# Gate products in two GpSimd steps, the next unit's normalisation at the iteration's end

## The reference, cut to what matters

```python
# block 0, per batch: m = silu(cond) @ w_ada + b_ada, split in nine shifts, scales and gates
h = ln(x) * (1 + sc_msa) + sh_msa
h = windowed_self_attention(h)                  # 16 heads of 16, windows of 128, rolled by 64
x = x + h * g_msa
h = ln(x) * (1 + sc_mca) + sh_mca
h = topk_cross_attention(h, context)            # 77 context rows, softmax over the 16 largest scores of each head
x = x + h * g_mca
h = ln(x) * (1 + sc_mlp) + sh_mlp
a, b = split(h @ w_m1 + b_m1)                   # 1024 each
x = x + (silu(a) * b @ w_m2 + b_m2) * g_mlp
# block 1: layer norm, attention to 77 prototypes, three experts (silu), router, gate
nx = layer_norm(x); ev = softmax(nx Wq (P Wk)^T) P Wv
routed = sum_e p_e * (silu([nx, ev, anchor] @ e_w1) @ e_w2 + e_b2)
x = x + sigmoid(silu([nx, ev, anchor] @ gate_w1) @ gate_w2) * (routed @ out_w + out_b)
```

## Time and profile before

| what | value |
|---|---|
| timed runs | 1451.67, 1452.09, 1446.48 us (median 1451.67) |
| profiled execution | 1447.34 us, span 1445.5 us |
| busy: TensorE / its weight loads | 97% / 81% |
| busy: VectorE / ScalarE / GpSimd | 73% / 56% / 30% |
| chain that ended last | TensorE 59%, VectorE 31%, issue 5%, ScalarE 2%, GpSimd 1% |
| mean granted TensorE clock | 0.992 |
| spacing of the full iterations | 81.3 to 89.9 us |

### The profile page before, as it was taken

How to read it: one execution, slowest core, us unless ns; L and a number is a source line. 1 busy time by engine, 2 the same in 40 slices (tenths; PEclk the granted TensorE clock), 3 DMA queues, 4 the chain that set the end, 5 groups by cost and what they waited for, 6 DMA issues and landing times.

```text
span 1445.5 us, 29891 instructions
## 1 busy us (share of the span) xinstructions
PE 1402.6 (97%) x9585; PEld 1174.8 (81%) x9585; DVE 1061.5 (73%) x4754; ACT 815.8 (56%) x2523; POOL 439.9 (30%) x600
## 2 busy tenths in 40 slices
PE   7999999999999999999999999999999999999997
PEld 5878788888888788888888788888888878887886
DVE  3576869687786868879696787959688786968632
ACT  3473474747566375755647366564757547474433
POOL 1414132333224233332335132233334313232302
PEclk9999999999999999999999999999999999999999
DMA  7610000000010000010010000000010000000000
GB/s 244 207 64 2 1 8 19 9 27 9 20 32 16 1 2 25 1 34 9 19 33 1 16 1 16 11 23 13 8 34 19 16 2 7 3 1 9 1 2 14
DMA packets 32760, 35.29 MB, mean 24 GB/s; under 512 B 8744, under 2 KB 27868, under 8 KB 32349
## 3 DMA queue, kind: packets, MB, share of 16 engines
q1 hardware_dynamic: 32605, 33.38, 7.6%
HBM read 28.83 MB, written 4.22 MB: 23 GB/s over the span
## 4 chain that ended last, share of the span: by engine, by line
PE 59%; DVE 31%; issue 5%; ACT 2%; POOL 1%; SPq 0%; DMA 0%; DVEq 0%; POOLq 0%; ACTq 0%
PE bank L1033 10%; DVE knocked L2264 10%; PE bank L964 9%; PE bank L1009 7%; PE bank L824 6%; PE bank L1016 4%; DVE M L2257 4%; DVE M L2252 4%; PE bank L873 4%; PE bank L973 3%; PE bank L863 2%; PE bank L810 2%; DVE scores L2272 2%; PE bank L885 2%; DVE gT L2279 2%
## 5 line engine op out<-in xcount | busy, mean ns | idle before, releaser
L964 PE MATMUL bank<-hB,Wm 128*128 128x256 f32 x1024 | 244.0, 384 | 2.2 <-ACT hB L1404 2.2
L964 PEld LDWEIGHTS bank<-hB,Wm 128*128 128x128 f32 x1024 | 191.8, 191 | 33.8 <-issue 7.0
L1009 PE MATMUL bank<-nxT,W1nx 128*128 128x256 f32 x896 | 212.5, 383 | 0.0
L1443 ACT ACTIVATE prob<-bank,rmax 128x128 f32<-128x128 f32 x512 | 179.9, 435 | 28.1 <-DVE rmax L2191 28.1
L1801 POOL TENSOR_TENSOR scores<-scores,M 128x308 f32<-128x308 f32 x128 | 94.8, 741 | 318.4 <-DVE knocked L2264 317.1
L1033 PE MATMUL bank<-W2p,gT 128*128 128x256 f32 x768 | 183.2, 381 | 3.0 <-DVE acc L2343 1.9
L1009 PEld LDWEIGHTS bank<-nxT,W1nx 128*128 128x128 f32 x896 | 166.5, 191 | 23.2 <-issue 2.8
L1033 PEld LDWEIGHTS bank<-W2p,gT 128*128 128x128 f32 x768 | 141.2, 190 | 23.8 <-issue 2.8
L1493 ACT ACTIVATE tbs<-bank,b1half 128x256 f32<-128x256 f32 x128 | 60.6, 473 | 145.0 <-PE bank L964 103.9
L1443 ACT ACTIVATION_READ_ACCUMULATOR prob<-bank,rmax 128x1 f32 x512 | 140.7, 276 | 0.0
L1509 ACT ACTIVATE tbs<-bank,betaH 128x256 f32<-128x256 f32 x224 | 95.1, 486 | 80.1 <-PE bank L1016 79.1
(11 more groups left out here) (240 smaller groups left out, 2800.7 us busy)
## 6 DMA issues: line engine op xcount, KB each, us to landing
Wm_g<-in_L_xcond_w_m_dram SPq DMA_DIRECT2D x4, 1024.0 KB, 5.5
W1ev<-in_L_xcond_e_w_dram SPq DMA_DIRECT2D x6, 512.0 KB, 7.6
x<-in_x_dram SPq DMA_DIRECT2D x16, 128.0 KB, 2.5
x<-in_x_dram SPq DMA_DIRECT2D x32, 64.0 KB, 2.4
Wm<-in_L_xcond_w_m_dram SPq DMA_DIRECT2D x1, 2048.0 KB, 9.2
out_dram<-acc SPq DMA_DIRECT2D x16, 128.0 KB, 1.7
out_dram<-acc SPq DMA_DIRECT2D x32, 64.0 KB, 2.0
batch_rows<-row_store SPq DMA_DIRECT2D x4, 384.0 KB, 3.7
```

Of the source, the lines that this page charges most:

```text
L964: m = pe.matmul(bank_of(name)[:, half * UT:(half + 1) * UT], Wm1[:, k, c:c + P], hB[:, k, :], start=(k == 0), stop=(k == CB - 1))
L1009: pe.matmul(bank_of(name)[:, n * UT:(n + 1) * UT], W1nx[:, k, c0 + n * P:c0 + (n + 1) * P], nxT[:, k, :], start=(n == 0 and k == 0), stop= ...
L1443: m = act.activation(prob[:, s, i, :], psum[s][:, i * P:(i + 1) * P], ACT.Exp, bias=rmax[:, t, s * HPS + i:s * HPS + i + 1], accum_out=rsu ...
```

## The change

The first half of each gate product goes from one VectorE instruction to two on GpSimd (add 1 in place in `tb`, then multiply into `gT`), with a semaphore `tanh_raised` between them. The eight calls stand among GpSimd's bias adds and shifts. The kept sums are inverted and spread tile by tile, each as soon as its sum is there; the query biases move behind them. The first normalisation of unit a + 1 is done at the end of the iteration, in `xnA`, after TensorE has turned that buffer for ln2. ScalarE copies picked block (0,3) and takes the first kept exponential earlier. The prologue gains unit 2's normalisation.

```diff
@@ TensorE: a_turn_inverses
-                pe.wait_ge(spread if values == "pv" else spread_x, u + 1)
+                if values == "pv":
+                    pe.wait_ge(spread, u + 1)
-                for f in range(CB):
-                    for t in range(1 if values == "pv" and u >= 2 else TILES):
+                for t in range(1 if values == "pv" and u >= 2 else TILES):
+                    if values == "xv":
+                        pe.wait_ge(spread_x, u * TILES + (t + 1))
+                    for f in range(CB):
@@ ScalarE: both (last_cross alike)
                 a_copy_picked(0, 2, c)
+                a_copy_picked(0, 3, c)
                 b_proto_exp(b)
                 a_cross_exp(1, 0, c)
-                a_copy_picked(0, 3, c)
+                a_kept_exp(0, c)
                 a_copy_values(a)
                 b_copy_weights(b)
                 a_cross_exp(1, 1, c)
-                a_kept_exp(0, c)
@@ GpSimd: new functions
+            def a_spread_kept(t, u):
+                pool.wait_ge(kept_inverted, u * TILES + (t + 1))
+                pool.tensor_copy(kept[:, t], kinv[:, t, :].rearrange("p (h a) -> p h a", a=1).to_broadcast([P, H, D])).then_inc(spread_x, 1)
+            def b_half_gate(j, u):
+                name = f"m{j}"
+                pool.wait_ge(tanh_done, u * len(TANH_ORDER) + (TANH_ORDER.index(name) + 1))
+                w = tb[tb_of(name)][:, 0:UT]
+                pool.tensor_scalar(w, w, 1.0, None, ALU.add).then_inc(tanh_raised, 1)
+                pool.wait_ge(tanh_raised, u * HJ + (j + 1))
+                pool.tensor_tensor(gated_of(u)[:, j, :], w, gated_of(u)[:, j, :], ALU.mult).then_inc(half_gated, 1)
@@ GpSimd: prologue
-                a_spread("xv", 0)
+                a_spread_kept(0, 0)
+                a_spread_kept(1, 0)
                 rstd_of(1, EPS0, 1)
                 rstd_of(2, EPS0, 0)
+                rstd_of(0, EPS0, 2)
@@ GpSimd: both (last_cross alike; last_experts has the eight half gates after its bias add)
+                b_half_gate(0, b)
                 add_bias(1, xc, c)
                 a_shift(0, 0, c)
+                b_half_gate(1, b)
                 a_shift(0, 1, c)
-                rstd_of(0, EPS0, a)
+                b_half_gate(2, b)
+                a_shift(0, 2, c)
+                b_half_gate(3, b)
+                a_shift(0, 3, c)
+                b_half_gate(4, b)
+                b_half_gate(5, b)
+                b_half_gate(6, b)
+                b_half_gate(7, b)
                 if r == 3:
                     gate_so(batch)
                 if r == 0:
                     gate_co(batch)
-                a_shift(0, 2, c)
-                a_shift(0, 3, c)
                 add_bias(0, xa, a)
...
+                a_spread_kept(0, c)
                 a_shift_kept(1, c)
-                a_spread("xv", c)
+                a_spread_kept(1, c)
...
                 rstd_of(2, EPS0, c)
+                if a + 1 < NU:
+                    rstd_of(0, EPS0, a + 1)
                 rstd_of(1, EPS0, a)
@@ VectorE: helpers
-            def a_invert_kept(u):
-                dve.wait_ge(kept_sum, u * TILES + TILES)
-                dve.reciprocal(kinv[:, :, :], ksum[:, :, :]).then_inc(kept_inverted, 1)
+            def a_invert_kept(t, u):
+                dve.wait_ge(kept_sum, u * TILES + (t + 1))
+                dve.reciprocal(kinv[:, t, :], ksum[:, t, :]).then_inc(kept_inverted, 1)
@@ b_swiglu
-                dve.wait_ge(tanh_done, u * len(TANH_ORDER) + (TANH_ORDER.index(name) + 1))
-                dve.scalar_tensor_tensor(gated_of(u)[:, j, :], tb[w][:, 0:UT], 1.0, gated_of(u)[:, j, :], ALU.add, ALU.mult).then_inc(half_gated, 1)
                 dve.wait_ge(half_gated, u * HJ + (j + 1))
@@ VectorE: end of the prologue
                 ln_apply(2, xs[0], xnB, 0)
+                a_load(2, 0)
+                ln_stats(0, xs[2], 2)
+                wait_full(dve, "ln2", 1)
+                ln_apply(0, xs[2], xnA, 2)
@@ VectorE: both
-                a_load(ra, batch)
-                ln_stats(0, xa, a)
...
-                wait_full(dve, "ln2", a - 1)
-                ln_apply(0, xa, xnA, a)
...
                 a_topk("b", 1, 2, c)
+                a_pick(1, 0, c)
+                a_sum_kept(0, c)
+                a_invert_kept(0, c)
                 a_topk("b", 1, 3, c)
-                a_pick(1, 0, c)
+                a_pick(1, 1, c)
+                a_sum_kept(1, c)
+                a_invert_kept(1, c)
                 a_bias_queries(a)
-                a_pick(1, 1, c)
-                a_sum_kept(0, c)
-                a_sum_kept(1, c)
-                a_invert_kept(c)
...
                 ln_apply(2, xc, xnB, c)
+                if a + 1 < NU:
+                    a_load((r + 2) % UNITS, (a + 1) // UNITS)
+                    ln_stats(0, xn, a + 1)
                 a_values_out(oT, a)
...
                 b_mix(2, b)
+                if a + 1 < NU:
+                    wait_full(dve, "ln2", a)
+                    ln_apply(0, xn, xnA, a + 1)
                 b_finish(b, xb)
```

More of the change, by code:

```diff
@@ L310, in bass_pixart_experts @@
         tanh_done, half_gated, gated = sem("tanh_done"), sem("half_gated"), sem("gated")
+        tanh_raised = sem("tanh_raised")
         proto_max, proto_exp, proto_steps = sem("proto_max"), sem("proto_exp"), sem("proto_steps")
@@ L1812, in a_spread @@
             def a_spread(values, u):
[L1814 to L1819, removed]
-                alone(pool)
-                for t in range(1 if values == "pv" and u >= 2 else TILES):
-                    i = pool.tensor_copy(each[values][:, t], inv[:, t, :].rearrange("p (h a) -> p h a", a=1).to_broadcast([P, H, D]))
-                i.then_inc(spread if values == "pv" else spread_x, 1)
+                pool.wait_ge(sums_inverted, u + 1)
+                alone(pool)
+                for t in range(1 if u >= 2 else TILES):
+                    i = pool.tensor_copy(each[values][:, t], rinv[:, t, :].rearrange("p (h a) -> p h a", a=1).to_broadcast([P, H, D]))
+                i.then_inc(spread, 1)
+            def a_spread_kept(t, u):
+                pool.wait_ge(kept_inverted, u * TILES + (t + 1))
+                pool.tensor_copy(kept[:, t], kinv[:, t, :].rearrange("p (h a) -> p h a", a=1).to_broadcast([P, H, D])).then_inc(spread_x, 1)
             def gate(w, n, b, done):
@@ L1986, in last_experts @@
                 add_bias(2, xs[b % UNITS], b)
+                for j in range(HJ):
+                    b_half_gate(j, b)
                 rstd_of(3, EPS1, b)
@@ L2453, in prologue @@
                 a_sum_kept(0, 0)
+                a_invert_kept(0, 0)
                 read_fold("p21", W2p[:, 2 * RB + 2:2 * RB + 4, :].rearrange("p k c -> p (k c)"), fold_psum("p21")[:, :])
@@ L2463, in prologue @@
                 a_sum_kept(1, 0)
-                a_invert_kept(0)
+                a_invert_kept(1, 0)
                 a_normalise("pv", oT, 1)
@@ L2475, in prologue @@
                 ln_apply(2, xs[0], xnB, 0)
+                a_load(2, 0)
+                ln_stats(0, xs[2], 2)
+                wait_full(dve, "ln2", 1)
+                ln_apply(0, xs[2], xnA, 2)
             def both(k, r, batch):
                 a, c, b = k + 1, k, k - 1
-                ra, xa, xc, xb = (r + 1) % UNITS, xs[(r + 1) % UNITS], xs[r], xs[r - 1]
+                xn, xa, xc, xb = xs[(r + 2) % UNITS], xs[(r + 1) % UNITS], xs[r], xs[r - 1]
                 b_swiglu(0, b)
```

1 line of the change is left out of this document (removed).

## The result

The change makes the kernel 4.5% slower: 1514.1 us, the median of four runs (1506.58 to 1519.65), against 1449.7 for the kernel before on the same chip; ratio 1.0447, 95% interval 1.0422 to 1.0473. I had forecast 1448 and a range up to 1457. The profiled executions are 1519.65 (span 1517.9) and 1447.34 (span 1445.5), 72.3 apart; 64.9 of it lies in the 14 full iterations, 3.7 ahead of them and 3.7 behind them.

What follows compares the result with a forecast made beforehand. TensorE, 97% busy, bounds the kernel, waiting where VectorE runs solid. Full iterations -3.2, first +3.1, tail +0.4 sum to +0.3 us, or -2.2 without pick contention; -1 taken from 1449.4 gave 1448, range 1439 to 1457.

Steps and rivals of the forecast that it cites:

- the query biases end some 2.5 later than before, 422.8 against a need at 425: VectorE's query biases, moved behind sums and inverses, would end at 422.8, before their need at 425; no cost counted.
- the price of a gate: GpSimd's two steps per gate: 0.40 for the add, 0.74 for the product, 0.1 wait; 1.25 us, ends 1.2 and 1.6.
- TensorE's products for m1 to m6 keep over 0.5 of slack: With gates on GpSimd, TensorE's products for m1 to m6 would keep over 0.5 us of slack; only gate 7 remains.
- the clock: TensorE at half clock after a wait in the first iteration: 0 to 3.4 us more, 1.7 taken.
- the first iteration: Prologue's GpSimd gates Wm2 later, so TensorE waits about 2.0 us near 131, then half clock: +3.1 us.
- the tail behind the full iterations: Gate 7 comes 0.8 later in the second last iteration, costing +0.4 us; the last iteration costs 0.
- the pick's contention: Pick (0,0) on VectorE meets GpSimd's two-input steps: 0 to 0.7 us, 0.3 taken for r=0, 2, 3.
- the inverses' wait: TensorE's wait for cross attention's spread inverses, 14 times, 6.1 us in all; inverses ready 1.2 earlier would end it.
- The wait ahead of the transposes of pick (0,1): TensorE's wait for VectorE's pick (0,1), ahead of line 934: 0.7 to 1.0 us where r is 0 or 2.
- Gate 7's shift: VectorE's second m7 step starts 1.31 us after the tanh pass: +0.49 (r=0), +0.41 (r=2), -0.17 (r=3), 0 (r=1).
- Rival 2: GpSimd's gate 7 becomes the bound at 1.6 a gate and 0.7 of contention: +13 us, 1462; chance 0.16.
- earlier by the query biases less the first sum and reciprocal: -0.2: On VectorE, pick (1,1) would end 0.2 us earlier: query biases (0.78) leave, the first sum and reciprocal (0.6) come ahead.

Runs made afterwards that it cites:

- e4: The kernel before with only the query biases moved behind pick (1,1), the sums and the reciprocal: 1464.5 us, ratio 1.0116.
- e1: The changed kernel with the query biases put back behind pick (1,0): 1482.4 us, ratio 1.0241 to the kernel before.
- e6: e1 with both steps of gates 4 and 7 given back to VectorE, the other six gates on GpSimd: 1454.8 us, ratio 1.0050.
- e9: e1 with GpSimd's add of the constant replaced by a copy of the tile onto itself, leaving out the 1: 1457.3 us, ratio 1.0056.
- e3: The changed kernel with gates back on VectorE and query biases back behind pick (1,0): 1446.4 us, ratio 0.9992.
- e10: e7 with GpSimd's last kept shift put ahead of the first tile's spread: 1439.7 us, ratio 0.9933.
- e7: e3 with VectorE's last search and both picks put ahead of the sums and reciprocals: 1483.8 us, ratio 1.0252.

## Why the prediction was wrong

**The step that failed first** is "the query biases end some 2.5 later than before, 422.8 against a need at 425". I priced it by who reads the queries. The step also empties a bank, and the next writer of that bank are the transposes of pick (1,0), at 420.45 in the earlier trace rows. By the prediction's own numbers that gives a stop of 422.8 - 420.45 = 2.35 in each of 14 iterations; 2.02 to 2.22 was measured, 29.6 us in all, where the prediction had nothing. It needed only the list of bank uses beside the order on VectorE. e4 and e1 show this cause by itself.

**The second** is the price of a gate. The copy (0.40) was "the nearest" row for adding a constant, and the two-input operation (0.74) "above it". It was neither: 0.85. The bracket was argued by the number of inputs and no row excluded a dearer one-input arithmetic step. The Trainium skill, page "GPSIMD Engine Reference" (section 3.1, Elementwise — side-by-side cycle accounting), has one-input bodies well below the two-input operation's 2.6 cycles an element; this trace disagrees, with 0.85 for the one and 0.73 for the other at 256 columns.

**The third** is "TensorE's products for m1 to m6 keep over 0.5 of slack". For the products that is true in full iterations; m4's bank is next wanted by the turned tile, which the step didn't look at (14.0 us of waits). e6 and e9 show that it needed the mis-sized price as well: at 0.40 for the add there is no wait at m4's bank.

**The fourth** is the clock. I charged half clock to the first iteration and none to the others, as no stop over some 1.1 was forecast there. The stops of 2.0 to 2.2 us had it behind them eight times in 14, some 16 to 19 us.

**Smaller misses.** Gates at the real price cost the first iteration 4.2 us (94.3 in e1, 90.1 in e3) for the 3.1 forecast, and the tail behind the full iterations 3.4 (141.5 and 138.1) for 0.4. Without the pick's contention the sum should have been 3.0 lower (0.3 in ten iterations) and not 2.5. Neither touches the argument.

**Right:** the inverses' wait is gone. In the first iteration the stop was 2.34 us (2.0 forecast, 1.6 to 2.4) with half clock behind it. VectorE does wait for GpSimd at gates 4 and 7, 1.80 at m4 and 1.28 at m7, where 1.5 to 2 was forecast. The wait ahead of the transposes of pick (0,1) is 0.27 in its row and not 0.7 to 1.0, but by starts the normed tile and that pick together come 1.20 late where r is 0 (430.94 to 433.44 is 2.50, and the products between need 1.30), for the 1.07 forecast. Gate 7's shift follows the tanh pass: 1.31 forecast at a gate of 1.25, 1.30 in e9, and 1.78 at the real price of 1.68. The moved normalisation costs nothing; it gains some 3 us that I had not forecast apart. The pick's contention was 0.12 where r is 0 or 2 and 0.43 where r is 3, for the 0.3 taken; GpSimd's side lost 0.5. By the rule of the Trainium skill, page "SBUF — State Buffer" (Who interferes with whom), the pick would stand until the GpSimd step under way ends, which by these rows is 0.25 and 0.57, as an estimate; the trace has some 0.13 less each time.

**Rival 2** (slower, 1462) had half of it: gate 7 is late, by 1.78 - 0.82 = 0.96 where r is 0, and the first iteration pays, but gate 4, the biases and the clock of the other iterations were in none of my cases. With the biases back and the gate at my price, which is the world that I had forecast, e9 takes 1457, the upper end of my range and not its middle; most of what is left between them is pick (1,1), late by the sum and reciprocal ahead of it: e3, which has that wait and no GpSimd gates, is at 0.9992, and e10 without it at 0.9933. My step let the biases pay for it ("earlier by the query biases less the first sum and reciprocal: -0.2"), and behind pick (1,1) they cause the stop of 2.1.

**Open:** m4's bank was not given to another tile; why a stop of 2.15 halves the clock in one iteration and leaves it alone in the next isn't settled. The length of the stop alone doesn't decide it: stops of 1.67 had half clock behind nine of 14 in e7, stops of 1.61 to 1.81 behind three of 14 in e4, and those of 1.49 to 1.68 for m4's bank behind none of seven in the changed kernel and none of seven in e1.

## What to carry to other kernels

A step that reads a PSUM bank has two successors: who uses its result, and who next writes the bank. Before moving it, look up both, in the list of bank uses. An operation with no row of its own has no upper end from a dearer-looking one; where the queue is in order, multiply the price by the number of such steps behind one another. And when calls are exchanged on one engine, check the same pair on the engines that serve it: e7 and e10 differ by one exchange on GpSimd and by 44 us. A repeated stop can also cost more than its length: in e7 and in the changed kernel the half clock behind the stops took at least as much again.

## What the hardware showed that I had not expected

GpSimd adds a constant to a tile of 128 x 256 in 0.85 us, slower than it multiplies two such tiles (0.73), and copies one in 0.40. TensorE's clock fell to one half behind eight of 14 stops of 2.0 to 2.2 us, and behind none of the 28 stops for pick (1,1) in e1 and e3 (0.97 to 1.33 us); in e4, whose stops were 1.6 to 1.8 us, behind three, and in e7, at 1.67 us, behind nine. And filler products that TensorE executes during a stop paid: 1.7 us of useless products in each of 14 stops made the kernel 16 us faster.
